# Attention kernel: high and low part of v summed in the same 65 columns by two products

## The reference, cut to what matters

```
q, k, v = split_heads(x @ Wq.T), split_heads(x @ Wk.T), split_heads(x @ Wv.T)
sim  = einsum('bhid,bhjd->bhij', q, k) * scale
e    = exp(sim - max(sim)); attn = e / (sum(e) + EPS)
out  = einsum('bhij,bhjd->bhid', attn, v)
x    = x + out.reshape(B, N, INNER) @ Wo.T + bo
x    = x + ffn(layernorm(x))       # fp4 blocks of 16, silu(gate) * up, down
```

## Time and profile before

| what | value |
|---|---|
| median of three runs | 1464.04 us |
| the profiled execution's own time | 1464.06 us |
| its span (first to last instruction) | 1462.2 us |
| busy: TensorE, weight loads, VectorE, ScalarE, GpSimd | 1380.1, 892.1, 1101.9, 1137.5, 1245.4 us |
| granted TensorE clock, mean | 0.977 of full |
| HBM read and written | 4.80 and 2.10 MB |

### The profile page before, as it was taken

How to read it: one execution, slowest core, us unless ns; L and a number is a source line. 1 busy time by engine, 2 the same in 40 slices (tenths; PEclk the granted TensorE clock), 3 DMA queues, 4 the chain that set the end, 5 groups by cost and what they waited for, 6 DMA issues and landing times.

```text
span 1462.2 us, 35256 instructions
## 1 busy us (share of the span) xinstructions
PE 1380.1 (94%) x13828; PEld 892.1 (61%) x13828; DVE 1101.9 (75%) x1717; ACT 1137.5 (78%) x2413; POOL 1245.4 (85%) x1391
## 2 busy tenths in 40 slices
PE   4899999998999999999999999999999999999965
PEld 2466665665666666666666666666666666666644
DVE  7767677677678878787887868788786878878567
ACT  3798888976888878788887878888787878878822
POOL 5798989987998988898898889899888989989932
PEclk8999999999999999999999999999999999999958
DMA  7111111111111102112111211211121121112000
GB/s 175 45 45 45 45 36 32 35 33 44 45 45 34 38 23 49 45 45 49 34 38 23 48 45 44 49 38 34 24 48 45 45 49 40 32 23 49 2 4 15
DMA packets 46660, 59.77 MB, mean 41 GB/s; under 512 B 8672, under 2 KB 21920, under 8 KB 46496
## 3 DMA queue, kind: packets, MB, share of 16 engines
q1 hardware_dynamic: 46336, 57.26, 16.8%
q10 hardware_dynamic: 160, 0.26, 0.1%
HBM read 4.80 MB, written 2.10 MB: 5 GB/s over the span
## 4 chain that ended last, share of the span: by engine, by line
PE 65%; DVE 20%; POOL 6%; ACT 5%; issue 3%; DMA 1%; SPq 0%; DVEq 0%
PE ob L635 16%; PE st L606 12%; PE st L608 10%; PE sm L587 8%; DVE negm L941 7%; POOL p_low L450 5%; PE mb L523 4%; PE mb L539 4%; PE mb L528 2%; PE mb L1242 2%; PE mb L534 2%; ACT probs L761 1%; DVE v L909 1%; DVE qv L1115 1%; DVE hidden L1119 1%
## 5 line engine op out<-in xcount | busy, mean ns | idle before, releaser
L450 POOL TENSOR_TENSOR p_low<-probs 128x512 f16<-128x512 f32 x1024 | 1083.0, 1076 | 148.2 <-ACT probs L761 145.1
L761 ACT ACTIVATE probs<-st,lift,exp_scale 128x512 f32<-128x512 f32 x1024 | 792.2, 779 | 172.4 <-PE st L608 159.9
L941 DVE TENSOR_REDUCE negm<-sm 128x1 f32<-128x1024 f32 x508 | 617.6, 1216 | 105.4 <-PE sm L587 104.2
L606 PE MATMUL st<-q_hl,k_hh 128*128 128x512 f16 x1024 | 394.7, 385 | 2.3 <-DMA q_hm<-m_low 2.3
L608 PE MATMUL st<-q_hm,k_l 128*128 128x512 f16 x1024 | 389.4, 380 | 0.0
L635 PEld LDWEIGHTS ob<-v,probs 128*128 128x128 bf16 x4096 | 279.3, 98 | 123.1 <-ACT oscl L775 1.0
L635 PE MATMUL ob<-v,probs 128*128 128x129 f16 x4096 | 322.4, 222 | 0.6 <-ACT oscl L775 0.5
L635 PEld LDWEIGHTS ob<-v,p_low 128*128 128x128 f16 x4096 | 195.7, 98 | 127.7 <-POOL p_low L450 8.7
L587 PE MATMUL sm<-k_hh,q_hl 64*128 64x512 f16 x508 | 197.5, 389 | 23.1 <-DVE negm L941 23.0
L635 PE MATMUL ob<-v,p_low 128*128 128x65 f16 x4096 | 211.2, 195 | 5.4 <-POOL p_low L450 5.3
L587 PE MATMUL sm<-k_hh,q_hm 64*128 64x512 f16 x508 | 197.7, 389 | 0.0
(11 more groups left out here) (175 smaller groups left out, 1539.1 us busy)
## 6 DMA issues: line engine op xcount, KB each, us to landing
k_hh<-k_high SPq DMA_DIRECT2D x128, 128.0 KB, 2.4
k_l<-k_low SPq DMA_DIRECT2D x64, 128.0 KB, 2.3
q_hl<-q_high SPq DMA_DIRECT2D x64, 128.0 KB, 2.3
q_hl<-q_low SPq DMA_DIRECT2D x64, 128.0 KB, 2.4
q_hm<-q_high SPq DMA_DIRECT2D x62, 128.0 KB, 2.3
x<-x SPq DMA_DIRECT2D x4, 512.0 KB, 7.3
q_hm<-m_high SPq DMA_DIRECT2D x128, 1.0 KB
q_hm<-m_low SPq DMA_DIRECT2D x128, 1.0 KB
```

Of the source, the lines that this page charges most:

```text
L450: return pool.tensor_tensor(p_low[b][:, j, :], p, p.bitcast(BF16)[:, 1::2], ALU.subtract)
L606: pe.matmul(st[s % 2][:, :], k_hh[n][:, s * P:(s + 1) * P], q_hl[n][:, half * HALF:(half + 1) * HALF], start=True, stop=False)
L761: nc.scalar.activation(probs[k % 2][:, s, :], st[s % 2][:, :], ACT.Exp, bias=lift[:, 0:1], scale=exp_scale[:, head, pair:pair + 1]).then_i ...
L941: nc.vector.tensor_reduce(negm[k % 2][:, s // 2:s // 2 + 1], banks[:, :, :].rearrange("p a n -> p (a n)"), AX.X, ALU.max, negate=True).the ...
```

## The change: what it does

The row of `v` is laid out as two parts of 65: (1, v high) and (0, v low). The product of the high part of p is made by two matmuls of 65 columns instead of one of 129; both add to the same 65 columns of the bank. The low part of p is multiplied with (1, v high) as before. The bank so holds the finished sum, and ScalarE scales 64 columns for each tile directly to `o_n`. GpSimd's join, the buffer `oscl` and the semaphore `s_on` are gone; `s_ob` now tells both that the bank was read and that `o_n` is written.

```diff
-VC = 1 + 2 * DH
-VL = 1 + DH
+VC = 1 + DH
...
-        v = [sb(f"v{n}", [P, JT, 2, VC + 1], F16) for n in range(2)]
+        v = [sb(f"v{n}", [P, JT, 2, 2, VC], F16) for n in range(2)]
...
-                        if s == 2 and (prev if k < 2 else cur):
-                            join(g, q, k, 1)
-                        if s == 6 and (prev if k < 1 else cur):
-                            join(g, q, k, 0)
...
-            def join(g, q, k, bank):
-
-                at, pq, head, t = output_of(g, q, k, bank)
-                o = oscl[bank][:, :, :]
-                wait(pool, s_ob, at + 1)
-                pool.tensor_tensor(o_n[pq][:, t:t + 2, head * DH:(head + 1) * DH], o[:, :, 0:DH],
-                                   o[:, :, DH:2 * DH], ALU.add).then_inc(s_on, 1)
...
-                    wait(pe, s_on, 8 * (g - 1) - 2 * (1 - c))
+                    wait(pe, s_ob, 8 * (g - 1) - 2 * (1 - c))
...
-                                n = VL if low else VC
-                                last = pe.matmul(ob[bank][:, o:o + n], p, v[pq][:, j, ph, 1:1 + n],
-                                                 start=(j == 0 and s % 4 == 0), stop=(j == JT - 1 and low == 1),
-                                                 skip_group_check=True)
+                                sums = ob[bank][:, o:o + VC]
+                                last = pe.matmul(sums, p, v[pq][:, j, ph, 0, :], start=(j == 0 and s % 4 == 0),
+                                                 stop=(j == JT - 1 and low == 1), skip_group_check=True)
+                                if not low:
+                                    last = pe.matmul(sums, p, v[pq][:, j, ph, 1, :], start=False, stop=False,
+                                                     skip_group_check=True)
...
             def scaled(g, q, k, bank):
 
-                at = output_of(g, q, k, bank)[0]
+                at, pq, head, first = output_of(g, q, k, bank)
                 wait(act, s_nr, at + 1)
-
-                wait(act, s_on, at - 1)
                 for t in range(2):
-                    last = nc.scalar.activation(oscl[bank][:, t, :], ob[bank][:, t * OT + 1:t * OT + VC], ACT.Copy,
-                                                scale=rden[:, bank, t:t + 1])
+                    last = nc.scalar.activation(o_n[pq][:, first + t, head * DH:(head + 1) * DH],
+                                                ob[bank][:, t * OT + 1:t * OT + VC], ACT.Copy, scale=rden[:, bank, t:t + 1])
                 last.then_inc(s_ob, 1)
...
-                nc.vector.memset(v[n][:, :, :, 1:2], 1.0).then_inc(s_init, 1)
+                nc.vector.memset(v[n][:, :, :, 1, 0:1], 0.0).then_inc(s_init, 1)
+                nc.vector.memset(v[n][:, :, :, 0, 0:1], 1.0).then_inc(s_init, 1)
```

More of the change, by code:

```diff
@@ L202, in build @@
         rden = sb("rden", [P, 2, 2])
-        oscl = [sb(f"oscl{n}", [P, 2, 2 * DH]) for n in range(2)]
         o_n = [sb(f"o_n{n}", [P, TB, 2 * DH]) for n in range(2)]
@@ L245, in build @@
         s_vh = sem("v_high_made")
-        s_ob = sem("o_taken")
+        s_ob = sem("o_normalised")
         s_v = sem("v_made")
@@ L256, in build @@
         s_pv = sem("pv_done")
-        s_on = sem("o_normalised")
         s_dn = sem("sums_taken")
@@ L557, in round_ @@
                 if r == 1:
-                    pe.wait_ge(s_init, 4)
+                    pe.wait_ge(s_init, 6)
                     pe.wait_ge(s_k1, 4)
@@ L697, in take @@
                     wait(act, mb_ready[JOBS[m][1]], ready)
-                    nc.scalar.activation(v[1 - q][:, 4 * c:4 * c + 4, :, 2:2 + DH],
+                    nc.scalar.activation(v[1 - q][:, 4 * c:4 * c + 4, :, 0, 1:VC],
                                          bank[:, :].rearrange("p (t h d) -> p t h d", t=4, h=2), ACT.Copy).then_inc(s_vh, 1)
@@ L906, in take @@
                 elif name[0] == "v":
-                    part = v[1 - q][:, 4 * c:4 * c + 4, :, :]
+                    part = v[1 - q][:, 4 * c:4 * c + 4, :, :, 1:VC]
                     wait(dve, s_vh, 2 * g + c + 1)
-                    nc.vector.tensor_tensor(part[:, :, :, 2 + DH:2 + 2 * DH], bank[:, :].rearrange("p (t h d) -> p t h d", t=4, h=2),
-                                            part[:, :, :, 2:2 + DH], ALU.subtract).then_inc(s_v, 1)
+                    nc.vector.tensor_tensor(part[:, :, :, 1, :], bank[:, :].rearrange("p (t h d) -> p t h d", t=4, h=2),
+                                            part[:, :, :, 0, :], ALU.subtract).then_inc(s_v, 1)
                 elif name[0] == "n":
```

## The result

The changed kernel takes 1468.09 us (median of 12 runs, 1466.24 to 1469.27) against 1465.58 for the kernel before beside it (12 runs, 1461.32 to 1467.06): ratio 1.0019, 95% interval 1.0011 to 1.0027. It is slower by some 2.8 us, not by the 7.9 forecast. The direction came as forecast, the size about a third.

What follows compares the result with a forecast made beforehand. From some 50 to 1390 us TensorE's streaming was taken to bound the kernel. On 1464.06 us: +16.3 (bursts) - 4.4 (joins) - 2.0 (clock) - 2.0 (VectorE's waits) = +7.9, so 1472.0 us, range 1459 to 1486.

Steps and rivals of the forecast that it cites:

- The high bursts, +16.3: TensorE: 16 matmuls of 65 columns at 31.1 ns make each of 512 high bursts 32 ns longer, +16.3 us.
- The strided load: TensorE's high bursts: loading bf16 weights with step two stays hidden behind 65 columns, so 31.1 ns a matmul.
- The rival of a slow long burst: Loads or issue set the pace of TensorE's long bursts: +37 us (1509), at most +207 us (1671); chance 0.09.
- The end of the rounds, -1.9 and -2.0 for the clock: Last low burst: four joins fewer ahead of it save 1.9 us; TensorE's clock falling later saves 2.0.
- GpSimd's early waits, the other part of the -4.4: TensorE's other waits for GpSimd's low parts, in first and third round: 2.2 us plus a little saved.
- VectorE's waits take up a little: TensorE's 55 waits for maxima, 23.0 us, absorb some of the longer bursts: -2.0 us, bounds 0 and 3.5.
- The bound on the relief: Removing GpSimd's joins saves at most 14.0 us, the waits of TensorE and of its weight loads together.
- GpSimd's relief decides: Rival: GpSimd's lateness spaces the low bursts; without joins 1448.8 us, middle 1456; faster, chance 0.12.
- GpSimd's busy time: Profile sign on GpSimd: busy near 1125 us, with more idle time behind ScalarE.
- ScalarE's 15 to 35 us less: Profile sign on ScalarE: scaling 64 columns instead of 128 makes its busy time 15 to 35 us less.

Runs made afterwards that it cites:

- e2: Kernel before with its 129-column bursts, but only the high columns scaled straight to `o_n`, no joins, product with v low left out of the output: 1450.23 us, ratio 0.9897.
- e1: Kernel before with only the high bursts split into 16 matmuls of 65 columns, v low to columns of its own, joins kept: 1472.95 us, ratio 1.0050.
- e0: The kernel before once more, unchanged, for a second profile: 1464.15 us, ratio 1.0001.
- e8: Kernel before with VectorE's quantisation of `w_down` moved from round 8 to round 9: 1459.73 us, ratio 0.9963.
- e9: Kernel before with GpSimd's bias addition of round 7 moved three units earlier, quantisation left in round 8: 1459.16 us, ratio 0.9963.

## Why the prediction was wrong in size

- **The high bursts, +16.3: near, but not as it was worked out.** A pair takes 63.2 ns (29.4 and 33.8) where 62.2 was forecast, against 57.8 for a matmul of 129 columns where 58.3 was read, so a burst costs 43 ns more to the next group, not 32: 22 us in 512. The low bursts, put at no change, are 6 ns shorter, -3 us. The waits for maxima then take up 2.5 us of this without the joins (e2 against the changed kernel, rounds 9 to 31) and 3.9 with them (e1). What is left is 0.49 us a round or 15.7 in all between e2 and the changed kernel, where the forecast had 16.3 - 2.0; the agreement is in part luck. The strided load is hidden for the most part: the step to new weights is 33.8 ns, with f16 weights 30.5. The rival of a slow long burst had no part.
- **The end of the rounds, -1.9 and -2.0 for the clock: right in size.** 4.1 us in the last 75, with the clock at full until the rounds are over. But 1.1 of them also lie between the two profiles of the kernel before: against e0 it is 3.0, against e8 and e9 2.6.
- **GpSimd's early waits, the other part of the -4.4: right in size.** The changed kernel is ahead by 0.7 us when round 1 begins, which the loading ahead of it makes (e0 differs by as much), and by 0.9 when round 5 begins, in spite of four rounds of longer bursts, some 2 us. TensorE waits 1.5 us for the low parts instead of 5.3.
- **"VectorE's waits take up a little", -2.0, bounds 0 and 3.5: wrong.** This is the step that failed. It took the 23.0 us in 55 waits as 55 alike races between VectorE and TensorE's slots. One of them was 4.6 us, the row said so the earlier trace rows, and it was no race: VectorE was held up beside GpSimd. With what the slow clock behind it costs, taking it away is worth 5.1 to 5.3 us (e8 and e9 from the start of round 8), about 5.4 by the ratios. The other waits took up nothing in all, 18.5 us before and 19.9 after, for what the longer bursts took from them came back without the joins, beside the 44-number instructions. Without the stall on either side the sum comes near: the changed kernel against e8 is 1.0019/0.9963 = 1.0056 (1.0041 to 1.0071, from the two intervals), or +8.2 us, where +7.9 was forecast. That is why it was 2.8 and not 7.9.
- **The clock in rounds 5 and 7: no term of the sum.** The slow stretches there cost the changed kernel 3.2 us beside the first profile of the kernel before and e8, and 1.6 beside e9. The spans differ by 11.0 us from e8 and by 9.4 from e9; less these steps it is 7.8 both times. Against the first profile of the kernel before, with the stall's 5.3 us put back, it is 3.9 + 5.3 - 3.2 = 6.0. That these lie so close to 7.9 is luck too: bursts and waits were both off, in opposite directions.
- **The bound on the relief was too low as well.** "14.0 us, the waits of TensorE and of its weight loads for GpSimd" counts only waits that name GpSimd (and adds the idle times of two queues that overlap), and my value for all relief by the joins was 6.4. e2 gave 15, some 5 of them in the stall's round. The rival "GpSimd's relief decides" was right that relief is more than the waits for GpSimd, and wrong in its mechanism: lateness that spaces the low bursts can be worth no more than the 1.8 us that e2 wins evenly after round 8.
- **Small readings.** GpSimd's busy time was forecast at 1125 us and is 1151.6: the joins leave, but 94 us net, not 120.5, for consecutive GpSimd instructions overlap in the records (the low part of 338.79 begins before the join from 338.38 to 338.85 ends), so that a join adds less than its own 471 ns. ScalarE's 15 to 35 us less: 23.9. The rival of a slow pace adds its 37 us to 1472 and its 207 us to 1464, two bases for one mechanism.

What stays open: why the instruction misses the first end of a GpSimd instruction in one case and gets through in another. The 22 numbers of e9 and of the kernel before stood in line behind a low part that had 884 and 830 ns to go, and only the latter missed. That GpSimd's being behind has a part in it is shown by moving the bias addition and no other way, and it isn't enough by itself, as the 0.28 and 4.69 us at the end of the rounds show. That the stall lasts until GpSimd is out of work is seen in ten of eleven.

## What to carry to other kernels

Look at the longest of a group of waits and follow it through the waiting engine's own rows; a small VectorE instruction that takes thirty times its neighbour's time is itself a wait. The page names VectorE there and GpSimd nowhere, for the time is booked as busy. Before work is taken off GpSimd at TensorE's expense (here 16 us for 15), see whether moving one VectorE step away from the place where GpSimd is behind gives what one is after: here 5 us, for one number in a table. And an edit measured in two halves should have its halves added up: here they miss the whole by 10 us, which says that they share something, the wait between VectorE and GpSimd.

## What the runs showed of the hardware that I had not expected

- A TENSOR_SCALAR of 22 or 44 numbers a row took 3.8 to 5.3 us beside five or six GpSimd instructions with a join among them, and 0.18 to 0.99 us otherwise. The long ones may have ended by starving their own cause: with VectorE held, TensorE got no maxima, ScalarE no scores and GpSimd no probabilities, and in ten of eleven VectorE got through when GpSimd ran dry.
- A join between the low parts let the next such instruction through in 0.36 us where a low part held it for 0.99, in eleven rounds alike.
- The same program had TensorE's clock at 0.50 once ahead of a wait, at no cost, and once behind it, at a cost of 1.6 us (before and e0, round 7).
- Two profiles of one program repeated this to 7 ns (5.271 and 5.264 us).
- 65-column matmuls follow at 29.4 ns on the same weights loaded again and at 33.8 ns on the next ones (bf16 with step two), 30.5 with f16 weights of step one.
